# One activation per head for the score weights in a state-space stage, with the gate and the skip term moved

## The reference

```python
proj = u @ W_in.T                    # z, x, B, C, dt, A, trap, angles
Bh = rope(rmsnorm(B) + B_bias, theta); Ch = rope(rmsnorm(C) + C_bias, theta)
lam = sigmoid(trap); g = exp(a * dt)
def step(carry, inp):                # over the tokens
    h, bx_prev = carry
    bx_t = x_t[..., :, None] * B_t[..., None, :]
    h = g * h + dt * (lam * bx_t + (1.0 - lam) * g * bx_prev)
    y_t = einsum('bhpn,bhn->bhp', h, C_t)
    return (h, bx_t), y_t
y = (ys + D_param[:, None] * x) * silu(z)
return y @ W_out.T
```

## Time and profile before

| what | value |
|---|---|
| median of 3 runs | 2606.65 us (2595.26 to 2608.48) |
| the profiled execution, its own time | 2627.98 us |
| its span in the trace | 2626.1 us |
| the chunk stage in the span | about 1433 to 1722 us |

### The profile page before, as it was taken

How to read it: one execution, slowest core, us unless ns; L and a number is a source line. 1 busy time by engine, 2 the same in 40 slices (tenths; PEclk the granted TensorE clock), 3 DMA queues, 4 the chain that set the end, 5 groups by cost and what they waited for, 6 DMA issues and landing times. The chain is left out here.

```text
span 2626.1 us, 34853 instructions
## 1 busy us (share of the span) xinstructions
PE 2016.5 (77%) x10364; PEld 1043.8 (40%) x10364; DVE 1906.2 (73%) x2499; ACT 1415.1 (54%) x2505; POOL 1372.1 (52%) x995
## 2 busy tenths in 40 slices
PE   2587977979787776863974898964588898888877
PEld 1233333333333332531742677741135454444222
DVE  6199999999999998577168999965555655555652
ACT  1467767767776763531544444420356655755545
POOL 2198998988899997004023777733621111111553
PEclk9898989989898988877977999975689998999878
DMA  1244444444444543000130000011232333222111
GB/s 34 71 146 145 155 143 153 142 152 144 144 154 145 154 141 120 1 1 24 48 103 0 1 0 0 0 38 59 76 105 63 97 86 86 83 64 76 49 31 38
DMA packets 147098, 214.76 MB, mean 82 GB/s; under 512 B 30858, under 2 KB 58404, under 8 KB 146340
## 3 DMA queue, kind: packets, MB, share of 16 engines
q1 hardware_dynamic: 142868, 204.72, 25.8%
q0 software_dynamic: 4096, 8.40, 1.2%
HBM read 193.91 MB, written 23.86 MB: 83 GB/s over the span
## 5 line engine op out<-in xcount | busy, mean ns | idle before, releaser
L516 PE MATMUL ps<-m_hC,ident 128*128 128x512 f32 x1024 | 516.9, 650 | 129.3 <-DVE m_hC L798 129.3
L714 POOL TENSOR_TENSOR m_dBx<-m_du,m_rowB 128x1024 f32<-128x1024 f32 x256 | 603.7, 2384 | 7.4 <-DMA m_rowB<-bc_rows 7.1
L2478 DVE TENSOR_REDUCE a_mx<-ps 128x2 f32<-128x1024 f32 (+2 forms) x320 | 352.4, 1117 | 210.6 <-PE ps L2140 140.9
L2339 ACT ACTIVATE a_pT<-ps 128x512 f32<-128x512 f32 (+2 forms) x640 | 320.2, 553 | 306.9 <-PE ps L2162 263.1
L640 ACT ACTIVATE ps<-m_delta,m_A 128x512 f32<-128x512 f32 x512 | 339.7, 685 | 120.3 <-DVE m_h L789 119.4
L516 PEld LDWEIGHTS ps<-m_hC,ident 128*128 128x128 f32 x1024 | 205.5, 208 | 426.5 <-issue 235.5
L2625 POOL TENSOR_SCALAR_AFFINE_SELECT a_pT<-a_pT 128x512 f32<-128x512 f32 x128 | 81.4, 636 | 480.1 <-ACT a_pT L2339 478.8
L789 DVE TENSOR_TENSOR_SCAN m_h<-ps,m_carry,m_dBx 128x512 f32<-128x512 f32 x256 | 311.2, 1265 | 9.0 <-ACT ps L640 9.0
L789 DVE TENSOR_TENSOR_SCAN m_h<-ps,m_dBx 128x512 f32<-128x512 f32 x256 | 295.9, 1206 | 18.8 <-ACT ps L640 18.2
L798 DVE TENSOR_TENSOR m_hC<-m_h,ps 128x1024 f32<-128x1024 f32 x176 | 214.9, 1221 | 25.5 <-ACT ps L650 9.6
L724 POOL TENSOR_TENSOR m_hC<-m_h,m_rowC 128x1024 f32<-128x1024 f32 x80 | 194.2, 2428 | 73.1 <-DVE m_h L789 72.8
(11 more groups left out here) (366 smaller groups left out, 3797.7 us busy)
## 6 DMA issues: line engine op xcount, KB each, us to landing
m_rowB<-bc_rows SPq DMA_DIRECT2D x256, 256.0 KB, 4.4
m_rowC<-bc_rows SPq DMA_DIRECT2D x256, 256.0 KB, 3.9
a_w<-in_L3f_w1T SPq DMA_DIRECT2D x39, 256.0 KB, 2.5
a_w<-in_L3f_w2T SPq DMA_DIRECT2D x39, 256.0 KB, 3.3
qk_parts<-a_part SPq DMA_DIRECT2D x24, 256.0 KB
expert_rows<-in_zero_rows SPq DMA_DIRECT2D x39, 128.0 KB, 2.5
a_xs<-expert_rows SPq DMA_DIRECT2D x39, 128.0 KB, 2.2
expert_out<-a_y SPq DMA_DIRECT2D x39, 128.0 KB, 3.2
```

Source lines behind the costliest of these rows:

```text
L516: mm = pe.matmul(ps[:, bankY + c, :], k.ident[:], hC[:, n % NBUF, c, :], start=False, stop=n % NS == NS - 1)
L714: pool.tensor_tensor(dBx[:, n % NBUF], du[:, i % 2, :, chunk(i, x)], rowB[:, n % 4, :].unsqueeze(1).to_broadcast([P, HALF, CH]), ALU.mult) ...
L2339: act.activation(dst, src, ACT.Exp).then_inc(t_read, 1)
L2478: dve.tensor_reduce(mx[:, c % 2, :, es[0]:es[0] + len(es), t, x // CH], src, AX_X, ALU.max)\
```

## The change

It has three parts. The weights `wt` of a chunk, before two products over all heads on GpSimd, become four activations on ACT, one for each head (Identity, with scale `v` and bias `wdiag` per partition), placed behind `E`. The gate `g` on DVE moves from behind `cFe` to between `accept` and `n1` of the same step. The skip term is no longer x times `dI` for each head; the columns of W_in that give x are scaled by D once (`winD`), and a product of these with the normalized input gives the skip term for two heads at a time, over all 128 columns of the array, as the first of each pair's products.

```diff
-                step(dve.tensor_tensor(L["dI"][:], k.ident[:].unsqueeze(1).to_broadcast([P, H2, P]),
-                                       L["D"][:].unsqueeze(2).to_broadcast([P, H2, P]), ALU.mult), "dI")
+                step(dve.tensor_tensor(L["winD"][:], winT[:, X0:B0].rearrange("p (h n) -> p h n", h=H2),
+                                       L["D"][:].unsqueeze(2).to_broadcast([P, H2, HP]), ALU.mult), "winD")
...
-                def rotate(c, u, done):
+                def rotate(c, u, done, b):
...
                     if done is not None:
                         accept(done)
+                    if b is not None:
+                        gate(b, u)
                     when(dve, RG, "cd", c)
                     when(dve, RV, "ab", c)
                     RV.done(dve.tensor_tensor(v1, pa[:], pb[:], ALU.subtract), "n1")
+
+                def gate(b, u):
+                    when(dve, BT, "y", b)
+                    y = k.ps[:, yb, 0:2 * P].rearrange("p (a n) -> p a n", a=2)
+                    BV.done(dve.tensor_tensor(g[:, u], y, L["zs"][:, :, ds(b * P, P)], ALU.mult), "g")
...
                     if b is not None:
-                        when(dve, BT, "y", b)
-                        y = k.ps[:, yb, 0:2 * P].rearrange("p (a n) -> p a n", a=2)
-                        BV.done(dve.tensor_tensor(g[:, u], y, L["zs"][:, :, ds(b * P, P)], ALU.mult), "g")
                         when(dve, BT, "state", b)
...
-                        when(dve, RG, "wt", s)
+                        when(dve, RA, "wt", s)
...
-                        when(pool, SV, "M", r - 2)
-                        hold(k, pool)
-                        pool.tensor_tensor(wt[:, u], L["strict"][:].unsqueeze(1).to_broadcast(full), wide(L["v"], r),
-                                           ALU.mult).then_inc(k.wt_half, 1)
-                        pool.wait_ge(k.wt_half, r + 1)
-                        hold(k, pool)
-                        RG.done(pool.tensor_tensor(wt[:, u], wt[:, u], wide(L["wdiag"], r), ALU.add), "wt")
...
                         RA.done(act.activation(E[:, u], arg[:], ACT.Exp), "E")
+                        when(act, SV, "M", r - 2)
+                        for hd in range(H2):
+                            t = act.activation(wt[:, u, hd, :], L["strict"][:], ACT.Identity, scale=L["v"][:, ds(r, 1), hd],
+                                               bias=L["wdiag"][:, ds(r, 1), hd])
+                        RA.done(t, "wt")
...
-                            pe.matmul(o, x, M[:, u, hd, :], start=True, stop=False)
-                            pe.matmul(o, x, L["dI"][:, hd, :], start=False, stop=False)
-                            t = pe.matmul(o, H[:, hd, :], cFe[:, u, hd, :], start=False, stop=True)
+                            if hd % 2 == 0:
+                                pe.matmul(k.ps[:, yb, hd // 2 * P:hd // 2 * P + P], flat(L["winD"][:, hd:hd + 2, :]),
+                                          xns[:, u, :], start=True, stop=False, skip_group_check=True)
+                            pe.matmul(o, x, M[:, u, hd, :], start=False, stop=False, skip_group_check=True)
+                            t = pe.matmul(o, H[:, hd, :], cFe[:, u, hd, :], start=False, stop=True, skip_group_check=True)
```

More of the change, by code:

```diff
@@ L1230, in mamba3_gates_stage @@
         V = Steps(k, "dve", ["delta", *of("ss", "rs", "bcn")[:3 * early], "pre", "preA", "relu", "nabs",
-                             "pos", "neg", "tern", "weff", "dI", "sp", "u1", "u1b", "corr",
+                             "pos", "neg", "tern", "weff", "winD", "sp", "u1", "u1b", "corr",
                              *(f"ang{c}" for c in range(CPB)),
@@ L1489, in mamba3_chunks_stage @@
         RV, SV = Stream(k, "rope_dve", ["bch", "ab", "n1", "arg"]), Stream(k, "score_dve", ["cFe", "Q", "M"])
-        RA, SA = Stream(k, "rope_act", ["ta", "ebc", "E"]), Stream(k, "score_act", ["xn", "bF", "cF", "x"])
-        RG, SG = Stream(k, "rope_pool", ["cd", "n2", "wt"]), Stream(k, "score_pool", ["bw"])
+        RA, SA = Stream(k, "rope_act", ["ta", "ebc", "E", "wt"]), Stream(k, "score_act", ["xn", "bF", "cF", "x"])
+        RG, SG = Stream(k, "rope_pool", ["cd", "n2"]), Stream(k, "score_pool", ["bw"])
         RT, ST = Stream(k, "rope_pe", ["cum"]), Stream(k, "score_pe", ["x", "trB", "trC", "st"])
@@ L1554, in step @@
                     if r is not None:
-                        rotate(r, u, done)
+                        rotate(r, u, done, b)
                         argument(r, u)
-                    elif done is not None:
+                    else:
                         accept(done)
+                        gate(b, u)
                     if s is not None:
@@ L1613, in step @@
                         SG.done(pool.tensor_tensor(bw[:, 1 - u], bch[:, 1 - u, 0], wide(L["wb"], s), ALU.mult), "bw")
-                    if r is not None:
-                        when(pool, SV, "M", r - 2)
-                        hold(k, pool)
-                        pool.tensor_tensor(wt[:, u], L["strict"][:].unsqueeze(1).to_broadcast(full), wide(L["v"], r),
-                                           ALU.mult).then_inc(k.wt_half, 1)
-                        pool.wait_ge(k.wt_half, r + 1)
-                        hold(k, pool)
-                        RG.done(pool.tensor_tensor(wt[:, u], wt[:, u], wide(L["wdiag"], r), ALU.add), "wt")
                 pool.wait_ge(zero, 1)
@@ L1721, in layer2 @@
         L.update(winT=sb("winT", [P, SM0 + NSM]), woutT=sb("woutT", [P, 2, D]), weff=sb("weff", [P, D]),
-                 dI=sb("dI", [P, H2, P]), hbias=sb("hbias", [P, 2, H2, P]), bias=sb("bias", [1, D]),
+                 winD=sb("winD", [P, H2, HP]), hbias=sb("hbias", [P, 2, H2, P]), bias=sb("bias", [1, D]),
                  maskneg=sb("maskneg", [P, P]), strict=sb("strict", [P, P]),
@@ L1748, in layer2 @@
         mamba3_gates_stage(k, L)
-        k.wt_half = k.sem("c2_wt_half")
         mamba3_chunks_stage(k, L)
```

## The result

The changed kernel takes 2669.3 us (median of 4 runs, 2666.0 to 2672.1) against 2601.0 us for the kernel before in the same comparison (4 runs). The ratio is 1.026, 95% interval 1.022 to 1.030: 68 us slower. The forecast was 51 us more (2657 us), the range 2622 to 2682.

What follows compares the result with a forecast made beforehand. DVE was taken as the bound, TensorE close behind. A period 1.57 us longer over 29 periods (45.5 us), start-up 4.4, tail 1 and setup 0 sum to 51 us; on 2606.65 that gives 2657, range 2622 to 2682.

Steps and rivals of the forecast that it cites:

- The loop: Layer 2 chunks: `gate` ahead of `arg` closes a chain through ACT, PE and DVE; period 10.38 us instead of 8.81.
- The chunk at full clock: Chain from the end of one `arg` to the next, before any clock allowance: 3.50, 4.77 and 1.81, together 10.08 us.
- the longer `y`: PE, transposes to `state`: 3.27 us instead of 2.69, 0.58 us longer through turns between full and half width.
- the second head starts 0.28 behind the first: Layout of `y` on PE: the second head's half-width records start 0.28 us late, its last record 0.38 later.
- The clock: TensorE's 4.67 us on the chain, at the old granted clock of 0.94, take 0.30 us more per chunk.
- Rival 3: TensorE's clock falls to 0.86, costing 0.76 us instead of 0.30; period 11.0 us, 70 us slower, 2677; chance 0.10.
- Start-up and tail: Ends of the chunk stage: 4.4 us more up to `arg` of chunk 2, 1 us more in the tail.
- Rival 1: Chain does not close in time, DVE stays the bound, relieved: period 7.63 us, 34 us faster, 2573; chance 0.06.
- Rival 2: Chain closes cheaply: `wt` 1.17 us, `y` no longer, full clock; period 9.14 us, 13 us slower, 2620; chance 0.14.
- Rival 4: Identity and Exp share no ACT table: one loaded twice per chunk at 1.28 us, over 80 us more; chance 0.02.

Runs made afterwards that it cites:

- run 1: Changed kernel with the gate back behind `cFe`, weights on ACT and `winD` kept: ratio 0.997, period 8.37 us.
- run 2: Changed kernel with the weights back on GpSimd as two products, gate ahead and `winD` kept: ratio 1.002, period 8.69 us.
- run 6: Changed kernel with the four weight activations on ACT moved ahead of `E`, gate ahead and `winD` kept: ratio 1.000, period 8.77 us.
- run 8: Kernel before with only the weights changed, computed on ACT ahead of `E`: ratio 0.991, 2592.9 against 2617.2 us.
- skip_back: Changed kernel with `dI` and its four half-width products back in place of `winD`: ratio 1.034, mean period 11.50 us.
- run 9: Kernel before with only the gate moved ahead of `n1`: ratio 1.003, period 9.07 us.
- run 7: Changed kernel with the weights on ACT ahead of `E` and the gate back behind `cFe`, `winD` kept: ratio 0.993, period 8.14 us.
- run 4: Changed kernel with nine unused 128x128 products per chunk on PE ahead of its wait for `ta`: 2633.9 us, ratio 1.014.
- run 5: Changed kernel with `dI` back in place of `winD` and nine unused PE products ahead of the wait for `ta`: ratio 1.009.

## Why the prediction was right, and where its sizes were off

- **The loop.** The chain from one `arg` to the next is closed by the gate and carries `wt`. The rows after show it link by link. Run 1 opens it (the gate), runs 2 and 6 leave it closed and take `wt` out of it (another engine, another place); each took the loss away. DVE waits 2.9 us before `g` (3.2 forecast), PE 2.3 us before `cum` (about 2), the new activations take 479 ns (0.48), `cFe` 0.68 (0.7), `n1` 0.42 (0.43).
- **The chunk at full clock.** 9.80 us against 10.08. The failing term is the longer `y`: from the transposes to `state` it is 2.80 us, 0.11 more than before, not 0.58 more. The step that failed is "the second head starts 0.28 behind the first", taken from the old order. In the new order both heads of a pair run at once from the start: the eight half records between two full ones take

```profile
1572.66 0.39 PE L1689 MATMUL ps<-c_xn,l_winD 128*128 128x128 f32 x2
1572.98 0.45 PE L1691 MATMUL ps<-c_M,c_x 128*64 128x128 f32 x4
1573.25 0.40 PE L1692 MATMUL ps<-c_cFe,c_H 128*64 128x128 f32 x4
1573.57 0.49 PE L1689 MATMUL ps<-c_xn,l_winD 128*128 128x128 f32 x2
```

  0.59 us from their first start to the next full record, where 0.86 was laid out, twice per `y`. Two latencies were a little longer than forecast: `gate` starts 0.23 behind `state` (0.10), `cum` 0.14 behind `ta` (0.05). 10.08 - 0.47 + 0.13 + 0.09 = 9.83.
- **The clock.** This is the term that was mis-sized most. "At 0.94 it takes 0.30 us more" kept the clock of the kernel before. It fell to 0.88, and the mean period is 1.04 us above that of an undisturbed chunk. That is 29 x 0.74 = 21 us too little in the forecast. The chunk at full clock, 0.28 us too long in it, gave 8 us of this back. So the total came as near as it did partly by luck: with the shorter `y` and the clock of before, the same sum would have said some 43 us. Rival 3 had the clock about right (0.86 by a straight line over PE's busy share; 0.88 measured at 80%) but not its price, 0.76 us. Both shared the low-clock time out evenly over the period. In the trace it falls on the chain: PE idles, the chain reaches `cum`, and there the clock is low.

```profile
1588.50:1590.00 1.50, 0.00 (x0) 0.00 (x0) 1.40 (x2) 1.50 (x6) 0.00 (x0) 0.79 0.00 0
1590.00:1592.00 2.00, 1.99 (x3) 0.96 (x4) 1.49 (x3) 0.07 (x1) 1.69 (x3) 0.50 0.00 0
1592.00:1594.00 2.00, 2.00 (x9) 1.71 (x8) 0.00 (x0) 0.70 (x2) 1.71 (x2) 0.50 0.00 0
1594.00:1597.00 3.00, 3.00 (x23) 2.27 (x22) 0.00 (x0) 1.34 (x3) 0.00 (x0) 0.64 0.00 0
1597.00:1600.00 3.00, 3.00 (x26) 2.65 (x23) 2.65 (x9) 0.74 (x2) 0.00 (x0) 1.00 0.00 0
```

- **Start-up and tail.** From the first to the third `arg` it took 20.3 us instead of 14.2, 6.1 us more (4.4 forecast); the tail behind the last `arg` is unchanged (1 forecast). 29 x (10.84 - 8.81) + 6.1 = 65.0 us, the 64.9 of the stage; the forecast of 51 is short of it by 21 - 8 + 2 - 1 = 14 us.
- **Rival 1** was right about the relief and wrong about its reach: with the chain out of the way (run 8) the period is 8.09 and not 7.63 us, since with the gate in its old place `n1`'s wait for GpSimd stays.
- **Rival 2** was near the truth on `y` (0.11 us longer) but not on `wt` (1.54 us from the first of the four to `ta`, not 1.17) nor on the clock.
- **Rival 4** did not come: in the stage of the changed kernel, with Copy, Exp and Identity in turn, the lines view shows one table load.

```profile
L1640 ACT ACT_TABLE_LOAD x1 | 1.3, 1283 | 0.0
```

The Trainium skill, TensorEngine Tiling (Array Packing), section Key Properties, says that a change of tiling mode drains TensorE. The trace agrees in kind: the turns cost what the rows of before gave, about 0.1 us each, but were largely paid for by the better overlap within a pair.

Left open: by which rule `skip_back`, with a shorter `y` and the same idle stretch, gets a lower clock than the changed kernel. Runs 2 and 9, which differ in the skip term alone, show the same: clock 1.00 and period 8.69 us with `winD`, 0.95 and 9.07 with `dI`. Runs 7 and 8 do not: both have the full clock. Runs 4 and 5 show that filling the idle stretch removes the low clock in both, not why the two forms differ.

## What to carry to other kernels

In a pipeline written out by hand, an instruction's place is a dependency: before moving one forward, follow what it waits for back through every in-order queue, and add up the chain until it comes back to an instruction behind the new place. If the sum exceeds the bound engine's own work, the move costs the difference in every round, however much it relieves that engine. Work taken over by another engine belongs where that engine idles, not ahead of what the others wait for: with the gate left alone, the same activations ahead of `E` gained 0.9% (run 8). The gate's move gained nothing in any of three pairs of kernels. It cost some 74 us with the weights behind `E` (the changed kernel against run 1), 22 us with them ahead of `E` (run 6 against run 7), and 6 us with them on GpSimd (run 9 against the kernel before).

## What the runs showed of the hardware

- An idle stretch on PE costs twice. With 2.3 us of idleness per chunk the granted clock of the stage was 0.88, with stretches at 1.2 GHz that began within 1 us of PE's resuming; nine unused products per chunk in that stretch held it at 2.4 GHz, and the kernel with more work was 35 us faster. The Trainium skill, TensorE: Matmul & The Clock Gate, Part 1, says that TensorE's clock is gated by how busy it has been; the runs agree.
- Two chains of half-width products on the two halves of the array overlapped fully when each head had four records behind a full-width product: the record starts of the two heads lie 0.01 us apart in the changed kernel. With six records per head and no full-width product between, in the kernel before, the second chain started 0.28 us behind the first, once per `y`.
- DVE's product `cFe`, with two SBUF inputs, took 1.48 instead of 0.68 us beside GpSimd's `wt` products, reversibly: runs 2 and 8 show both values for the same instruction.
